# Cross attention and mixture of experts on one core: squares in two halves from GpSimd and VectorE, the key's chain a step later, weighed sums in pairs, one GpSimd loop

## The reference

```python
x = x + xattn(layernorm(x), ctx, Wq, Wk, Wv)      # x, ctx: (4, 512, 512)
x = x + ffn(layernorm(x), ...)

# xattn: 32 heads of 16
q = rmsnorm(heads(x @ Wq.T)); kv = concat([ctx @ Wk.T, ctx @ Wv.T]).reshape(b, m, 32, 16, 2)
k = rmsnorm(heads(kv[..., 0])); v = heads(kv[..., 1])
out = softmax(q @ k.T * 16 ** -0.5) @ v           # rmsnorm(t) = t * rsqrt(mean(t * t) + 1e-6)

# ffn: 7 routed experts, 2 per token, and a shared one; width 512
probs = softmax(top 2 of xt @ Wr + br + gate_bias)
u = xt @ Wup + bup; g = silu(u @ Wgate + bgate) * u; eo = g @ Wdown + bdown
out = sum over the experts of probs * eo, plus the same of the shared expert
```

## Time and profile before

| what | value |
|---|---|
| median of 3 runs | 972.75 us (972.32 to 972.9) |
| the profiled execution | 973.43 us, its span 971.7 us |
| mean granted TensorE clock | 0.996 |
| TensorE busy | 946.0 us, 97% of the span |
| VectorE busy | 707.2 us, 73% |
| ScalarE busy | 497.8 us, 51% |
| GpSimd busy | 208.4 us, 21% |

### The profile page before, as it was taken

How to read it: one execution, slowest core, us unless ns; L and a number is a source line. 1 busy time by engine, 2 the same in 40 slices (tenths; PEclk the granted TensorE clock), 3 DMA queues, 4 the chain that set the end, 5 groups by cost and what they waited for, 6 DMA issues and landing times.

```text
span 971.7 us, 17895 instructions
## 1 busy us (share of the span) xinstructions
PE 946.0 (97%) x6676; PEld 682.0 (70%) x6676; DVE 707.2 (73%) x1459; ACT 497.8 (51%) x619; POOL 208.4 (21%) x226
## 2 busy tenths in 40 slices
PE   8999999999999999999999999899999999999995
PEld 6634444454434543446999889799999999999995
DVE  7798767886678767885978787665867686858654
ACT  4588668866787658887324223322424243424221
POOL 1011000311012200321300001333233333233331
PEclk9999999999999999999999999999999999999998
DMA  9400100101101110324413114633544536635533
GB/s 330 169 1 23 65 1 1 45 33 39 61 1 44 45 66 1 110 75 163 176 44 112 65 56 144 204 65 54 178 80 123 131 77 193 187 66 157 117 56 41
DMA packets 32512, 87.42 MB, mean 90 GB/s; under 512 B 7744, under 2 KB 7744, under 8 KB 28352
## 3 DMA queue, kind: packets, MB, share of 16 engines
q1 hardware_dynamic: 21920, 60.70, 17.8%
q0 software_dynamic: 10528, 25.87, 13.1%
HBM read 61.83 MB, written 24.72 MB: 89 GB/s over the span
## 4 chain that ended last, share of the span: by engine, by line
PE 83%; DVE 7%; DMA 4%; issue 3%; ACT 2%; POOLq 1%; DVEq 0%; POOL 0%; SPq 0%; ACTq 0%
PE z_ps L905 15%; PE y_ps L905 14%; PE u_ps L905 13%; PE o_ps L640 11%; PE scores L624 8%; PE bank_a L677 5%; PE bank_b L661 5%; PE bank_b L647 2%; PE xt_ps L917 2%; PE bank_a L647 2%; DMA out<-y_sb,target 2%; PE tr L706 1%; PE tr L700 1%; PE tr L695 1%; DMA xg<-xn_dram,index 1%
## 5 line engine op out<-in xcount | busy, mean ns | idle before, releaser
L1178 ACT ACTIVATE probs<-scores 128x2048 f32<-128x2048 f32 x128 | 240.7, 1880 | 64.1 <-PE scores L624 61.1
L905 PE MATMUL z_ps<-u_hi,w_sb 128*128 128x256 f32 x896 | 168.3, 285 | 0.7 <-DVE u_lo L1867 0.7
L905 PE MATMUL u_ps<-x_hi,w_sb 128*128 128x256 f32 x864 | 159.2, 282 | 0.0
L1208 ACT ACTIVATE u_hi<-u_ps,b_ug 128x256 fp32r<-128x256 f32 x108 | 45.4, 471 | 197.6 <-PE u_ps L905 176.3
L905 PEld LDWEIGHTS z_ps<-u_hi,w_sb 128*128 128x128 f32 x896 | 141.0, 190 | 2.1 <-DVE u_lo L1867 1.2
L905 PE MATMUL y_ps<-w_sb,g_hi 128*128 128x512 f32 x448 | 139.5, 392 | 0.2 <-DVE g_lo L1885 0.2
L905 PEld LDWEIGHTS u_ps<-x_hi,w_sb 128*128 128x128 f32 x864 | 135.7, 190 | 1.1
L640 PE MATMUL o_ps<-probs,v_sb 128*17 128x512 f32 x1024 | 134.7, 598 | 0.0
L905 PE MATMUL z_ps<-u_lo,w_sb 128*128 128x256 f32 x448 | 126.6, 282 | 0.0
L905 PE MATMUL u_ps<-x_lo,w_sb 128*128 128x256 f32 x432 | 122.0, 282 | 0.0
L1220 ACT ACTIVATE s_sb<-z_ps,b_ug 128x256 f32<-128x256 f32 x112 | 47.0, 472 | 103.4 <-PE z_ps L905 103.4
(11 more groups left out here) (248 smaller groups left out, 1596.3 us busy)
## 6 DMA issues: line engine op xcount, KB each, us to landing
w_raw<-w_all SPq DMA_DIRECT2D x27, 1024.0 KB, 7.7
ctx_raw<-ctx_t SPq DMA_DIRECT2D x4, 1024.0 KB, 6.8
out<-x_sb SPq DMA_DIRECT2D x16, 256.0 KB, 2.0
xg<-xt_dram POOLq DMA_DIRECT2D x14, 256.0 KB
x_sb<-x SPq DMA_DIRECT2D x1, 3072.0 KB, 17.2
xn<-x_t SPq DMA_DIRECT2D x12, 256.0 KB, 4.7
xn_dram<-xn SPq DMA_DIRECT2D x12, 256.0 KB, 2.1
xt_dram<-xt SPq DMA_DIRECT2D x6, 512.0 KB, 3.0
```

Of the source, the lines that this page charges most:

```text
L905: ins = nc.tensor.matmul(out_ps, stat[a], mov[b], start=(first and a + b == 0), stop=(last and a == 1), skip_group_check=True)
L1178: nc.scalar.activation(probs[:, t % 2], scores[:], ACT.Exp).then_inc(p_ready, 1)
L1208: last = nc.scalar.activation(u_hi[:, c, :], u_ps[:, b, a, :], ACT.Identity, bias=b_ug[:, par, 0, c:c + 1])
```

## The change

The fp32 sum of squares becomes two fp32r matmuls with a copy `blocks_r` of the blocks: GpSimd casts the squares to `sq_hi` (`squares_high`), VectorE subtracts (`squares_low`, tile `sq_lo`). The first two queries' and the first key's sums stay fp32. The key's chain stands later: its sum in TensorE's step 3 (was 2), `sums_k` in VectorE's step 3 behind `newton_q` (was 2), log and root in ScalarE's steps 4 and 5 (were 3 and 4), `first_root_k` in step 5, `newton_k` in step 6. The weighed sums are taken at the steps of `SUMMED`, mostly two behind one another, with three buffers of `probs`; the query's and key's halves have one buffer for two units in place of two, each written when the unit before has used it (`half_scored`). The turns are dealt out anew. Behind attention, the table's matmuls stand behind z and go into `xt_ps`, and GpSimd runs one loop over tiles, with the wait for a scatter's landing at the front of the next scatter.

```diff
-        probs = asb("probs", [P, 2, QUADS, SEQ])
+        probs = asb("probs", [P, 3, QUADS, SEQ])
...
-        k_hi, k_lo = (asb(n, [P, 2, 2, CTX], FP32R) for n in ("k_hi", "k_lo"))
+        q_st = asb("q_st", [P, 2, SEQ], FP32R)
+        k_hi, k_lo = (asb(n, [P, 2, CTX], FP32R) for n in ("k_hi", "k_lo"))
...
-        K_TURNS = {6: (0, 4), 7: (4, 5), 0: (5, 9), 1: (9, 12)}
-        Q_TURNS = {3: (0, 5), 4: (5, 9), 5: (9, 12)}
+        K_TURNS = {6: (0, 1), 7: (1, 6), 0: (6, 7), 1: (7, 12)}
+        Q_TURNS = {2: (0, 1), 3: (1, 3), 4: (3, 7), 5: (7, 12)}
+
+        SUMMED = {0: (-2, -1), 1: (), 2: (0, 1), 3: (2,), 4: (3,), 5: (), 6: (4, 5), 7: ()}
+
...
+            def squares_high(n, before):
+                if n:
+                    pool.wait_ge(tr_ready, TR_AT[before] + 1)
+                nc.gpsimd.tensor_copy(sq_hi[:], sq[:]).then_inc(sq_high, 1)
+
+            def squares_high_k(u):
+                pool.wait_ge(sqk_done, u + 1)
+                squares_high(halved_k(u), ("sum_q", u))
+
+            def squares_high_q(u):
+                pool.wait_ge(sqq_done, u + 1)
+                squares_high(halved_q(u), ("sum_k", u - 1))
 
...
+                    squares_high_k(u + 1)
                     root2_k(u + 1)
+                if u + 2 < UNITS:
+                    squares_high_q(u + 2)
                 if behind and g == 1:
...
-                pool.wait_ge(out_stored, 16 * TILES)
-                scatter(n - 1)
-
-            total = routed(pool, lambda j, par, nth, first: None, turn)
-            scatter(total + NA - 1, more=False)
+
+            pool.wait_ge(start_ready, 1)
+            total = bound(pool, ER)
+            gather(NA + 1)
+            pool.wait_ge(out_stored, 16 * TILES)
+            scatter(NA - 1)
+            with pool.Fori(1, total) as i:
+                gather(i + (NA + 1))
+                scatter(i + (NA - 1))
+            scatter(total + (NA - 1))
 
...
+            def sum_halves():
+                nc.tensor.matmul(tr[:], blocks_r[:], sq_hi[:], start=True, stop=False)
+                nc.tensor.matmul(tr[:], blocks_r[:], sq_lo[:], start=False, stop=True).then_inc(tr_ready, 1)
+
...
+                    sum_halves()
 
             def sum_k(u):
                 begin("tr", TR_AT, ("sum_k", u), tr_free)
-                pe.wait_ge(sqk_done, u + 1)
-                nc.tensor.matmul(tr[:], blocks[:], sq[:], start=True, stop=True).then_inc(tr_ready, 1)
+                if u < 1:
+                    pe.wait_ge(sqk_done, u + 1)
+                    nc.tensor.matmul(tr[:], blocks[:], sq[:], start=True, stop=True).then_inc(tr_ready, 1)
+                else:
+                    pe.wait_ge(sq_low, halved_k(u) + 1)
+                    sum_halves()
 
             def out_transposes(u, ab):
...
                         v_even(u)
-                    if u + 1 < UNITS and not (more and g == 2):
+                    if ahead and not q_late:
+                        q_turns(u + 2, *Q_TURNS[s])
+                elif s in Q_TURNS:
+                    if s == 3 and u + 1 < UNITS:
                         sum_k(u + 1)
-                elif s in Q_TURNS:
                     if ahead:
-                        q_turns(u + 2, *Q_TURNS[s])
+                        first, end = Q_TURNS[s]
+                        q_turns(u + 2, 0 if s == 3 and q_late else first, end)
                     if s == 3 and behind and g == 2:
...
                 elif s == 7:
                     if ahead:
+                        sum_q(u + 2)
                         k_turns(u + 2, *K_TURNS[s])
-                    if ahead:
-                        sum_q(u + 2)
 
             def after(u, s):
                 b, g, more, behind = batch_of(u)
                 if s == 2 and more and g == 2:
                     v_even(u)
-                    sum_k(u + 1)
...
-                    between(u, s)
-                    if u or s:
-                        weighed(STEPS * u + s - 1)
+                    if s in (3, 7):
+                        between(u, s)
+                    for back in SUMMED[s]:
+                        if u or back >= 0:
+                            weighed(STEPS * u + back)
+                    if s not in (3, 7):
+                        between(u, s)
                     after(u, s)
             first_up(5 * UP_TURNS, len(UPS))
             pe.wait_ge(p_ready, STEPS * UNITS)
-            weighed(STEPS * UNITS - 1)
+            for t in (STEPS * UNITS - 2, STEPS * UNITS - 1):
+                weighed(t)
 
...
+                at = xt_ps[:, 0].rearrange("p a n -> p (a n)")[:, 0:COLS]
                 for i in range(PART):
                     last = nc.tensor.matmul(at, hot_row[:, w * PART + i, :], hot_col[:, i, :],
                                             start=(i == 0), stop=(i == PART - 1))
...
-            tile(5, 0, behind_up=lambda: table_part(5, 0), windows=2, bounds=range(1, DC + 1))
-            tile(6, 0, behind_up=lambda: table_part(6, 1), windows=3, bounds=range(DC + 1, ER + 1))
+            tile(5, 0, behind_z=lambda: table_part(0), bounds=range(1, DC + 1))
+            tile(6, 0, behind_z=lambda: table_part(1), bounds=range(DC + 1, ER + 1))
...
+                if u == 1:
                     act.wait_ge(tr_ready, TR_AT["sum_q", u] + 1)
+                elif u:
+                    act.wait_ge(sq_low, halved_k(u))
...
-                elif s == 3:
+                elif s == 4:
                     if nxt:
                         log_k(u + 1)
-                elif s == 4:
+                elif s == 5:
                     if nxt:
                         root_k(u + 1)
-                elif s == 5:
...
-                        act.wait_ge(pv_done, t - 1)
+                    if t > 2:
+                        act.wait_ge(pv_done, t - 2)
                     elif t == 0:
                         act.wait_ge(w_split, W_AT["q1"] + 1)
-                    nc.scalar.activation(probs[:, t % 2], scores[:], ACT.Exp).then_inc(p_ready, 1)
+                    nc.scalar.activation(probs[:, t % 3], scores[:], ACT.Exp).then_inc(p_ready, 1)
             first_u_high(1)
             group_out(UNITS - 1, 1)
...
 
+            def squares_low(n):
+                dve.wait_ge(sq_high, n + 1)
...
+            def half_scored(u, ab):
+                if u:
+                    dve.wait_ge(sc_ready, STEPS * (u - 1) + MT * (ab + 1))
...
                         context_split(b + 1, 1)
+                    if nxt:
+                        squares_low(halved_k(u + 1))
                     if u == 0:
                         v_out(0, 2)
                     if more and g >= 2:
                         v_out(b + 1, 2 * g - 4)
-                    if nxt:
-                        sums_k(u + 1)
...
                 elif s == 3:
                     if nxt:
                         newton_q(u + 1)
+                        sums_k(u + 1)
...
                     if nxt:
-                        first_root_k(u + 1)
                         stack_q(u + 1, 0)
...
                     if nxt:
-                        newton_k(u + 1)
+                        first_root_k(u + 1)
                     finalize(u, 0)
                     if more and g >= 2:
                         v_out(b + 1, 2 * g - 3)
                 elif s == 6:
+                    if nxt:
+                        newton_k(u + 1)
+                    if u + 2 < UNITS:
+                        squares_low(halved_q(u + 2))
+                    if nxt:
+                        stack_k(u + 1, 0)
                     if more and g == 1:
                         x_low(b + 1, 0, DC + 2 * b + 1)
                         x_split(b + 1, 1)
-                    if nxt:
-                        stack_k(u + 1, 0)
                     if behind and g >= 2:
...
-            tile(5, 0, x_tile=10, during_u=lambda: hot_cols(0), before_x=lambda: table_out(0),
-                 during_y=lambda: hot_rows(1))
+            tile(5, 0, x_tile=10, during_u=lambda: hot_cols(0),
+                 during_y=steps_of(lambda: table_out(0), lambda: hot_rows(1)))
```

78 lines of the change are left out of this document (45 added, 33 removed).

## The result

| | before | changed |
|---|---|---|
| median | 972.55 us (4 runs, 972.32 to 972.9) | 1003.68 us (4 runs, 1002.38 to 1006.24) |
| profiled execution, its span | 973.43, 971.7 us | 1004.26, 1002.5 us |
| mean granted clock | 0.996 | 0.986 |
| attention (first scores of unit 0 to the last ones of unit 15) | 418.9 us | 456.7 us |
| behind and ahead of it | 552.8 us | 545.8 us |

The ratio is 1.0323 (95%: 1.0304 to 1.0341), so the changed kernel is 31 us slower. The forecast was 990 with a range to 1001. The last two lines of the table split the 30.8 us between the spans: attention lost 37.8 where I had put 24, the rest won 7.0 where I had put 6.9.

The account below looks back on a forecast made before the run. TensorE was taken to bound attention, ScalarE within 6%, with VectorE's written order between them. Span 971.7 + 24 (attention) - 7 (behind it) = 988.7, plus 1.05 to the median: forecast 990, range 974 to 1001.

Parts of the forecast that it names:

- TensorE's part: Attention, TensorE: two fp32r sums save about 0.5 twice a unit, a pair takes 1.85, a light unit 22.75 against 23.05.
- Light units behind a statistic: Attention, units 4, 5, 9 and 13: the log waits for `ssq`, 23.8 against 23.05, +0.7 us each.
- Units 6 and 10: Attention: late `ssk` makes step 3 6.25, late gate parts make step 7 4.5; 35.6 against 31.49, +4.1 each, +8.2.
- The others: Attention: unit 7 +3.7, 11 +1.9, 2 and 3 +0.85 and +1.55, 14 +2.2, 15 +1.4, 0 and 1 +2.3.
- Behind attention: Behind attention: two waits for `hot_col` go, -1.8; the second computed gather issues earlier, -5.1; together -6.9, taken as -7 us.
- GpSimd's cast: Attention, GpSimd: taken as 1.04 (bounds 1.04 and 2.33), hidden even at 2.1; at 2.33 some 5 us.
- Rival 1: Attention: VectorE's lateness is absorbed and only TensorE's work counts; -8 there, 957.7 in all; chance 0.13.
- the sum for attention: Attention, all units' gains and delays added up: +24 us.
- rival 4: Attention: more than the +24, as GpSimd's casts slow VectorE (9 us, 999) or stalls lower TensorE's clock (4 us); chance 0.15.

Follow-up runs that it names:

- `ssk` in front: Changed kernel with VectorE reading the key's sum (`ssk`) directly behind the values' copy, ahead of the statistics and the query's Newton step: 993.8 us.
- the halves alone: Changed kernel with the key's chain at its old steps and weighed sums one a step, keeping the two-matmul sums of squares: 982.3 us.
- x's halves early: Changed kernel with the low halves of x ahead of the key's first half in VectorE's step 6: 1012.6 us.
- the casts twice: Changed kernel with a second cast of the same size, which nobody reads, behind each of GpSimd's 29 casts: 1012.2 us.
- x's split late: Changed kernel with the third split of x moved from the end of step 7 to step 1 of the next unit, behind the output: 1004.1 us.
- late work back: Changed kernel with `ssk` read behind the values' copy, gate parts ahead of the key's halves, x's low halves and statistics behind the query's sum: 987.9 us.
- the key's chain early: Changed kernel with the key's sum, `ssk`, log, roots and Newton step back at their old steps on all engines: 986.2 us.
- none of the three parts: Changed kernel with sums in fp32, the key's chain at its old steps, and weighed sums one a step with the turns of before: 965.9 us.

## Why the prediction was wrong

The direction was right, and so was the main mechanism: readers of `tr` come late by VectorE's order, as the run with `ssk` in front shows. The size was not, and two terms of it had been put at nothing.

- **TensorE's part.** Right: a pair 1.84 (1.85), the two short matmuls 0.56 (0.46), units 8 and 12 at 22.67 and 22.68 (22.75). The pair also has the Trainium skill's rule on tiling modes (TensorEngine Tiling (Array Packing), Key Properties) on its side: the second group in the same mode pays no drain, and the trace agrees.
- **Light units behind a statistic.** Right: units 4, 5 and 9 +0.6 to +0.7 (0.7); unit 13 +1.4 (0.7).
- **Units 6 and 10.** Steps 3 and 7 right: 6.09 and 6.55 (6.25), 4.47 (4.5) in unit 6, but 5.54 in unit 10, where the clock had fallen within the step. The sum of the unit wrong: +7.4 and +8.9 where I had 4.1. Step 1 (2.9 forecast) was 4.71 and 4.21, since I followed `ssq` behind the splits of x but not `eps`, which stands behind them too, nor the transfer that a split waits for. Without the half clock in unit 6, steps 1 are 2.6 above the forecast for both units together, steps 0 (5.13 and 5.11, 4.6 forecast) 1.0, and steps 2 (5.5 forecast, 6.15 in unit 10) 1.3: some 5 us.
- **The others.** Units 7, 11 and 14 +4.9, +3.8 and +3.2 (3.7, 1.9 and 2.2), units 2 and 3 together +2.6 (2.4), unit 15 +1.4 (1.4), units 0 and 1 +3.0 (2.3).
- **Behind attention.** Right, -7.0 (-6.9).
- **GpSimd's cast.** 0.61, below my lower bound of 1.04. In the changed kernel it is hidden, as I had said (TensorE waits 0.5 for `sq_lo` in all); where the key's sum stands in step 2, as with the halves alone, it isn't. What it does to VectorE is 0.24 on the addition to x, and 0.29 on the few other instructions with two SBUF inputs that stand beside one. There are 29 casts, not 28.
- **Rival 1's sum** of -8 isn't what its terms give: 6 x 0.37 and 6 x 1.1 won and 2.3 lost are -6.5.
- **The step that failed** is the sum for attention, which kept the clock out. I had "a stall of 2.8 lowers TensorE's clock as the one of 3.99 did: 1.1 each for three to five, 4 us" as part of rival 4, which I gave 0.15. The runs showed five stretches that lost 1.7 to 3.4 each, 10.2 in all, behind waits of 1.6 to 3.1. The second term at nothing was the wait for `eps` in units 6 and 10, part of the 5 us above.

**What the 10.2 cost** can be told in part. Executions of one kernel differ in their granted clock, and with it in time. With x's halves early the fastest ran at 0.987 in 1003.9 us and the slowest at 0.976 in 1014.7: 11 us less lost, 11 us less time. With the casts twice it was 0.987 and 1006.4 against 0.980 and 1013.8: 7 and 7.5. Among the four executions of the changed kernel itself the two don't go together (0.991 took 1003.1, 0.987 took 1002.4). There I can only put a step beside the like step without a stretch, an estimate. Unit 0's stretch cost nothing: with x's split late it is absent, and step 1 of unit 1 starts at 69.27 where it was 69.32, since in both the log waits for `ssq`. Unit 6 lost 1.0 (steps 1 and 2 beside unit 10's), unit 7 1.3 (step 4: 4.04, and 2.79 with `ssk` in front), unit 10 1.5 (steps 3 and 4 beside unit 6's), and the double stretch 3.2 (step 7 of unit 10 beside unit 6's, step 0 of unit 11 beside 3.37 with `ssk` in front). That makes 7 of the 10.2. With it the account closes to within some 0.5 us that cancel between the other units: 24 forecast, 7 for the clock, 5 for steps 0 to 2 of units 6 and 10, and 1.8 for units 13 and 14 are 37.8. The last 1.8 I can't put down to one cause; in unit 13 there is a wait of 0.49 for `sq_lo`.

Forecasting stalls of 2 to 3 us in ten places, I had to count half clock behind about half of them; the forecast would have been 997, and with the late `eps` 1002. Which wait lowers the clock stays open: in the changed kernel the wait of 2.42 at 218.99 did not, that of 1.58 in front of the gate parts at 356 did. Nor is it shown why the run with late work back had no such stretch in its profiled execution.

## What to carry to other kernels

- Where one bank or buffer serves five uses in a written order, work out when each reader gets to its read in the fullest unit, not in the emptiest. Two light units here were 0.4 faster, the four light ones behind a statistic 0.6 to 1.4 slower, and four heavy ones lost 25 us.
- A cheaper operation on the bounding engine that needs two more engines ahead of it pays only where the whole chain (here 2.2 us) lies under other work.
- Price half clock behind forecast stalls of TensorE of the size seen here, and expect a wider spread between executions: 4 us for the changed kernel and 11 for the version with the most half clock, under 1 for the version with none of the three parts.

## What the runs showed of the hardware

- GpSimd's cast of 128x512 from fp32 to fp32r takes 0.610 (0.609 to 1.126), where its product of two such tensors takes 1.04 and its scaling 2.33.
- With casts beside it, a 128x256 addition of two SBUF tensors on VectorE took 0.662 in the median for 0.425. When the cast was doubled that median did not move, but ten 128x512 subtractions of two SBUF tensors took 0.98 for 0.69.
- A TensorE that waited 1.5 to 3.1 us was in five cases of eleven (changed kernel, attention) granted 1.2 GHz for 3 to 7 us afterwards, while fully busy again. In the run with the key's chain early a stretch stood behind a wait of 1.08. Taking one such wait away, by x's split late, moved the stretches to other places without changing their sum.
